# A loop of 13 turns over 56 edge steps on VectorE, or one of 22 turns over 32 steps with 24 steps in line behind it

## The chip, the cores and the metric

The kernel runs on one core of a Trainium2 chip. The metric is the device time of one execution in microseconds (us), lower is better. TensorE is written PE here, as in the profile, VectorE is DVE, ScalarE is ACT, GpSimd is POOL and SyncE is SP.

## The reference

The kernel computes two graph layers with residual normalization over 12500 nodes of 64 features and 400000 edges sorted by target node. Cut to what matters:

```python
def layer0(x, src, dst):                      # mean over in-edges, two small products
    mean = segment_sum(x[src], dst) / maximum(degree, 1)
    return relu(concat([x, mean]) @ W_fc + b_fc) + x @ W_res + b_res

def conv(x, edge_attr, src, dst):             # twice, with a relu between
    msg = x[src] @ Wm + bm + edge_attr @ We + be
    return segment_sum(msg, dst) + x @ Ws + bs

x = layernorm(x + layer0(x, src, dst))
x = layernorm(x + layer1(x, edge_attr, src, dst))   # layer1 = conv, relu, conv
```

Since `edge_attr @ We` is linear, the sum of the edge features over the edges of each node, `segment_sum(edge_attr, dst)`, is needed only once, 400000 rows of 64 floats. That sum is the stage that the change touches.

## The kernel before

The program runs in this order: preparation (the steps and tables are worked out on the chip), round 0 (neighbour sums for layer 0), the **edge sum**, and rounds 1 and 2 (the two convolutions). Each engine has its own instruction stream, written out by hand, with semaphores between them. An engine's sequencer works through the stream, does waits, register sums and branches itself, and hands the tensor operations to the engine.

The edge sum takes the edges in groups of 640 (128 partitions by 5), 625 groups, in 728 steps (`ESTEPS`); a group that reaches over a border of two blocks of 128 nodes takes a step for each block. The 8 buffers of a step's data turn round (`EB = 8`, `h` is the step modulo 8). One step passes through five engines:

- SP (L1540) loads 160 KB of edge features into `feats`.
- POOL (L1291) writes `rel_e`, the target node of each edge less the first node of the block.
- DVE (L921) compares it with a row of lane numbers and so marks, 128 by 640, which edge belongs to which node of the block (`mark_e`).
- ACT (L1416) turns the marks of two steps into floats (`hot_e`).
- PE (L1179) multiplies features by marks into one PSUM bank of 8, five products in a step.
- DVE (L932) adds the bank of the step six before (`LAG = 6`) to the block's sum in `sums_e`.

So DVE does two tensor operations in each step, L921 and L932. The block that L932 adds to is one of 98 and is known only at run time. `load_blocks` (L463 to L471) reads it into the sequencer's registers: one TENSOR_LOAD reads 32 bit words, each with four block numbers. In the stream one `load_blocks` stands ahead of every 16 steps (four words), and where fewer than 16 steps are left of the loop's body, for those alone (8 steps, two words).

The stage's loops on the other engines have 91 turns of 8 steps (PE, ACT, POOL) or 13 turns of 56 (SP, `TURNS = 7`). On DVE the loop (L913) has 13 turns of 56 steps. Behind it DVE adds the last six banks (L938), and PE then folds the sums (L1188). Every engine goes on to round 1 from there.

Of the kernel before, what the change touches and what calls it, by code (L numbers as in the profile page):

```python
# [105 lines left out]
def gnn_program(nc, step_c, first_row, x, src, dst, edge_attr, W_fc, b_fc, W_res, b_res,  # L106
# [26 lines left out]
    EB = 8  # L133
    LAG = 6
    EDGE0 = LAG % 4
    ESTEPS = -(-(GROUPS + BLOCKS - 1) // EB) * EB
    TURNS = 7
    assert ESTEPS % (EB * TURNS) == 0
    ES = -(-(ESTEPS + 1) // P)
    NB = 7  # L140
# [30 lines left out]
    with ctx:  # L171
# [291 lines left out]
        def load_blocks(frm, n):  # L463

            words = steps[0:1, :].bitcast(I32)
            _, packed = nc.values_load_multi_w_load_instructions(  # L466
                words[0:1, bass.ds(frm, n // 4)], engines=(ENG.DVE,), min_val=0,
                max_val=(BLOCKS - 1) * 0x01010101,
                skip_runtime_bounds_check_because="four block numbers, each clamped when the path was made")
            return [nc.s_assert_within(b, 0, BLOCKS - 1, skip_runtime_bounds_check_because="one of the four block numbers")  # L470
                    for v in packed for b in (v & 0x7F, (v >> 8) & 0x7F, (v >> 16) & 0x7F, v >> 24)]  # L471

        def flat(v):
            return v.rearrange("p b d -> p (b d)")
# [3 lines left out]
        def _(dve):  # L478
# [58 lines left out]
            for b in range(-(-CG // CH)):  # L537
                cols = slice(b * CH, min(b * CH + CH, CG))
                n = cols.stop - cols.start
# [90 lines left out]
            for b in range(3):  # L630
                cols = slice(b * GP, min(b * GP + GP, SG))
                n = cols.stop - cols.start
# [66 lines left out]
            for c0, c1, landed in ((0, SG // 2, s_g[0]), (SG // 2, SG, s_last)):  # L699
                dve.wait_ge(landed, 16 * (c1 - c0))  # L700
                n, cols = c1 - c0, slice(c0 * P, c1 * P)
# [25 lines left out]
            for r in range(3):  # L727
# [82 lines left out]
                if r == 0:  # L810
# [5 lines left out]
                    for b0, blocks, wd, deeps, s0 in REG:  # L816
                        upto, pair = steps_upto(wd, deeps)
                        many = at_once(wd)
                        with dve.Fori(0, blocks // 2) as i:
                            for j in range(2):  # L820
# [3 lines left out]
                                for q in range(upto[j][0], upto[j][WPB]):  # L824
                                    n, s = q % RING, bass.ds(i * pair + (q + s0), many)
# [11 lines left out]
                                    if part == 0:  # L837
                                        dve.wait_ge(b_used[j], it + (1 + j))
                                        if b0 < 2 * GI:
                                            bs = load_blocks((it * 2 + j) * (GW // 4), GW)  # L840
# [69 lines left out]

                step(V.memset(ps[:, EB - LAG:EB, 0:P], 0.0), "zeros_e")
                first_block = SETS * GW + GW + EDGE0 - LAG
                with dve.Fori(0, ESTEPS // EB, TURNS) as turn:  # L913
                    for n in range(EB * TURNS):
                        i, h = turn + n // EB, n % EB
                        if n % (2 * EB) == 0:
                            bs = load_blocks(turn * (EB // 4) + (first_block + n) // 4, min(2 * EB, EB * TURNS - n))
                        if h % 2 == 0:
                            dve.wait_ge(e_hot[h // 2], i + 1)
                        dve.wait_ge(e_rel[h], i + 1)  # L920
                        marks = V.tensor_tensor(mark_e[:, h, :, :].rearrange("p j (c u) -> p j c u", u=2),  # L921
                                                lane16[:, 0:P].rearrange("p (c u) -> p c u", u=2).unsqueeze(1)
                                                .to_broadcast([P, EG, P // 2, 2]),
                                                rel_e[:, h, :, :].unsqueeze(2).to_broadcast([P, EG, P // 2, 2]),
                                                ALU.is_equal)
                        if h % 2:
                            marks.then_inc(e_mark[h // 2], 1)
                        b = (h - LAG) % EB
                        dve.wait_ge(e_mm[b], i + (2 if h >= LAG else 1))
                        dve.wait_ge(e_add, i * EB + (h + EB))  # L930
                        to = flat(sums_e[:, bass.ds(bs[n % (2 * EB)], 1), :])
                        V.tensor_tensor(to, to, ps[:, b, 0:P], ALU.add).then_inc(e_add, 1)  # L932
                last = load_blocks((SETS * GW + ESTEPS + GW + EDGE0 - LAG) // 4, EB)
                for k in range(LAG):
                    dve.wait_ge(e_mm[EB - LAG + k], ESTEPS // EB + 1)
# [652 lines left out]
```

## Time and profile before

| | |
|---|---|
| median of 3 runs | 3590.3 us (3588.47 to 3590.58) |
| span of the profiled execution | 3585.2 us, from its first instruction to its last |
| busy in the span | PE 88%, DVE 65%, POOL 56%, ACT 45% |
| edge sum, first mark of DVE to its last | 1536.6 to 2020.2 us |
| TensorE's granted clock in the edge sum | 0.99 of full speed (2.4 GHz) |

The span leaves out what lies ahead of the first instruction and behind the last, so a run's time is some us longer than a span: the median is 5.1 us above this one. In the rows, `DVEq` is the sequencer of DVE: register sums (ALU_OP, FUSED_REGOPS), loads into registers (TENSOR_LOAD) and branches; while it does them no new tensor operation is handed to the engine. "issue" is time in which an engine waited for nothing that the profile shows. A name such as `union` is the memory in which several tiles lie in turn (`mark_e`, `hot_e` and `feats` in this stage); `abuf` holds `sums_e`.

### The profile page before, as it was taken

What the parts mean: (1) busy time and instruction counts of PE and PEld (TensorE: products, weight loads), DVE (VectorE), ACT (ScalarE), POOL (GpSimd) and SP (SyncE); (2) the same over time, 40 slices, a digit from 0 to 9 for tenths busy, and PEclk for the clock granted to TensorE, in tenths of its full rate; (3) what the DMA queues carried; (4) which work ended last, traced back from release to release, by engine and by line L of the source; (5) the groups of instructions that cost most, each with busy time, mean ns of one, the idle gap of its engine ahead of it and who ended that gap; (6) DMA issues with size and microseconds to landing.
All of it is one profiled execution on the core that took longest, in us unless ns stands there. A gap on an engine that the chain in (4) does not pass through costs nothing.

```text
span 3585.2 us, 114923 instructions
## 1 busy us (share of the span) xinstructions
PE 3167.6 (88%) x39408; PEld 2958.1 (83%) x39408; DVE 2339.3 (65%) x5369; ACT 1613.7 (45%) x2096; POOL 2021.8 (56%) x2292
## 2 busy tenths in 40 slices
PE   0239999999999999889999889999999889999995
PEld 0127988888888888778888879999999889999995
DVE  8779998888888888779999682333333423333335
ACT  0123677878999999788988650000000400000000
POOL 6761234445666666534444256666666666666664
PEclk9869999999999999999999979999999999999998
DMA  3521455556666666668888429999999599999996
GB/s 92 134 18 70 167 194 198 218 213 233 238 240 251 251 238 240 245 207 247 248 246 247 147 93 400 403 402 402 402 402 403 202 354 403 402 402 402 402 402 241
DMA packets 232872, 959.10 MB, mean 268 GB/s; under 512 B 44815, under 2 KB 144285, under 8 KB 173818
## 3 DMA queue, kind: packets, MB, share of 16 engines
q1 hardware_dynamic: 186027, 884.48, 65.0%
q0 software_dynamic: 46784, 73.84, 6.8%
q8 instruction: 33, 0.54, 0.1%
q14 instruction: 28, 0.23, 0.0%
HBM read 694.75 MB, written 263.40 MB: 267 GB/s over the span
## 4 chain that ended last, share of the span: by engine, by line
PE 68%; DVE 11%; issue 8%; POOL 6%; DVEq 3%; ACT 2%; DMA 2%; SPq 0%; ACTq 0%; POOLq 0%
PE ps L1109 48%; PE ps L1132 10%; DVE union L805 5%; PE ps L1179 4%; PE ps L1101 3%; POOL abuf L1213 3%; DVE union L921 2%; ACT union L1416 1%; DVE abuf L932 1%; POOL union L1213 1%; PE ps L1069 1%; DVEq L466 1%; DVEq L932 1%; PE ps L1188 1%; POOL abuf L1255 0%
## 5 line engine op out<-in xcount | busy, mean ns | idle before, releaser
L1271 POOL DMA_INDIRECT msg<-y_tab,idx x1368 | 1531.1, 1119 | 1041.9 <-ACT idx L1377 652.0
L1109 PE MATMUL ps<-union,abuf 128*128 128x192 bf16 x14896 | 1265.3, 247 | 13.9 <-DVEq L782 10.2
L1109 PEld LDWEIGHTS ps<-union,abuf 128*128 128x128 f16 x14896 | 1226.7, 98 | 21.2 <-issue 10.6
L1398 ACT ACTIVATE abuf<-ps 128x784 f16<-128x784 f32 x1216 | 1000.7, 823 | 239.9 <-PE ps L1132 212.3
L805 DVE TENSOR_TENSOR union<-lane,union 128x1568 f16<-128x1568 f16 (+3 forms) x1440 | 949.5, 710 | 31.0 <-PE ps L1132 27.1
L1109 PE MATMUL ps<-early,abuf 128*128 128x195 bf16 x7546 | 853.4, 249 | 0.0
L1109 PEld LDWEIGHTS ps<-early,abuf 128*128 128x128 f16 x7546 | 677.1, 99 | 100.9
L1132 PE MATMUL ps<-union 128*128 128x392 f16 (+2 forms) x4288 | 689.5, 288 | 52.4 <-DVE union L805 47.1
L1377 ACT ACTIVATE idx<-src_g 128x6 int32 (+1 forms) x228 | 46.4, 205 | 1280.2 <-PE ps L1101 1277.9
L1179 PE MATMUL ps<-union 128*64 128x128 f32 x7280 | 444.4, 278 | 48.2 <-ACT union L1416 48.1
L1179 PEld LDWEIGHTS ps<-union 128*64 128x64 f32 x7280 | 394.1, 137 | 98.4 <-DVE abuf L932 79.2
L1416 ACT ACTIVATE union<-union 128x1280 f32<-128x1280 f16 x364 | 432.9, 1259 | 55.9 <-DVE union L921 53.9
L797 DVE TENSOR_TENSOR acc<-acc,ps 128x64 f32 (+1 forms) x918 | 203.7, 222 | 364.2 <-DVE acc L797 211.2
L1132 PEld LDWEIGHTS ps<-union 128*128 128x128 f16 x4288 | 362.9, 108 | 92.3 <-issue 48.3
L921 DVE TENSOR_TENSOR union<-lane,rel_e 128x640 f16<-128x640 f16 x728 | 352.5, 484 | 41.7 <-issue 40.3
L1291 POOL TENSOR_TENSOR rel_e<-early,base_e 128x10 f16 x728 | 208.4, 305 | 287.5 <-DVE union L921 271.1
L880 DVE TENSOR_REDUCE part_d<-ps 128x64 f32<-128x192 f32 x152 | 54.4, 358 | 459.2 <-PE ps L1109 459.2
L786 DVE TENSOR_TENSOR hot_g<-code_g,lane 128x768 f16<-128x768 f16 x228 | 218.0, 956 | 70.2 <-DVE acc L797 69.2
L932 DVE TENSOR_TENSOR abuf<-abuf,ps 128x128 f32 x728 | 203.5, 280 | 1.8 <-PE ps L1179 1.1
L1101 PE MATMUL ps<-msg,hot_g 128*128 128x64 bf16 (+1 forms) x4104 | 167.2, 194 | 5.5 <-DMA msg<-y_tab,idx 5.5
L1101 PEld LDWEIGHTS ps<-msg,hot_g 128*128 128x128 f16 x4104 | 157.0, 98 | 6.0 <-DMA msg<-y_tab,idx 6.0
L854 DVE TENSOR_TENSOR acc<-acc,ps 128x65 f32 x456 | 99.5, 218 | 56.8 <-DVE acc L854 37.9
(229 smaller groups left out, 1241.4 us busy)
## 6 DMA issues: line engine op xcount, KB each, us to landing
abuf<-a_dram SPq DMA_DIRECT2D x304, 1568.0 KB
a_dram<-abuf SPq DMA_DIRECT2D x76, 3136.0 KB
union<-in_edge_attr_dram SPq DMA_DIRECT2D x728, 160.0 KB, 2.9
msg<-y_tab,idx POOLq DMA_INDIRECT x1368
y_tab<-union SPq DMA_DIRECT2D x28, 336.0 KB, 2.2
abuf<-in_x_dram SPq DMA_DIRECT2D x28, 224.0 KB, 3.4
y_tab<-early SPq DMA_DIRECT2D x7, 682.5 KB, 5.5
out_dram<-union SPq DMA_DIRECT2D x2, 800.0 KB, 3.5
```

The costliest lines, as they stand in the source:

```text
L786: V.tensor_tensor(hot_g[:, j * G:(j + 1) * G, :], code_g[:, bass.ds((it * 2 + j) * G, G)].unsqueeze(2).to_broadcast([P, G, P]), lane16[:, ...
L805: return V.tensor_tensor(to.rearrange("p s (c u) -> p s c u", u=2), lanes.unsqueeze(1).to_broadcast([P, n, width // 2, 2]), codes[:, which ...
L921: marks = V.tensor_tensor(mark_e[:, h, :, :].rearrange("p j (c u) -> p j c u", u=2), lane16[:, 0:P].rearrange("p (c u) -> p c u", u=2).uns ...
L932: V.tensor_tensor(to, to, ps[:, b, 0:P], ALU.add).then_inc(e_add, 1)
L1101: last = nc.tensor.matmul(tile_ps(r, j, k), hot_g[:, s, :], msg[:, s, c * width_of[r]:(c + 1) * width_of[r]], start=c == 0, stop=c == 2)
L1109: last = nc.tensor.matmul(ps[:, bank, 0:3 * width_of[r]], abuf[:, buffer, hi * P:(hi + 1) * P], ycols[r][:, hi, :], start=hi == 0, stop=hi ...
L1132: nc.tensor.matmul(ps[:, w % 4, 0:WIN].rearrange("p (h d) -> p h d", d=WD)[:, :, d0:d0 + wd], hot_c[:, n, WIN:WIN + P], hot_c[:, n, 0:HIS ...
L1179: last = nc.tensor.matmul(ps[half:half + D, h, 0:P], feats[:, h, j * D:(j + 1) * D], hot_e[:, h, j, :], start=j < 2, stop=j >= EG - 2)
L1271: pool.indirect_dma_start(msg[:, s, 0:3 * width_of[r]], None, y_tab[r], bass.IndirectOffsetOnAxis(ap=idx[:, s:s + 1], axis=0)).then_inc(ga ...
L1291: nc.gpsimd.tensor_tensor(rel_e[:, h, :, :], flat(dst_e[:, bass.ds(grp[h], 1), :]).unsqueeze(2) .to_broadcast([P, EG, 2]), base_e[:, bass. ...
L1398: A.activation(abuf[:, j, :].rearrange("p (h w d) -> p w h d", w=WPB, d=WD) [:, w:w + 2, :, :], ps[:, w % 4:w % 4 + 2, 0:WIN].rearrange("p ...
L1416: A.activation(hot_e[:, h:h + 2, :, :], mark_e[:, h:h + 2, :, :], ACT.Copy)\
```

## The change

The body of the DVE loop becomes a function of a first turn and a number of turns of 8 steps. The loop now takes 4 such turns (`HELD`), 32 steps, and goes round 22 times; the 24 steps that are left stand behind it in line, with numbers in place of registers where the turn is known. The steps themselves, their order and their semaphores stay as they are, on DVE and elsewhere; SP keeps its body of 56 steps.

```diff
     TURNS = 7
+    HELD = 4
...
-                with dve.Fori(0, ESTEPS // EB, TURNS) as turn:
-                    for n in range(EB * TURNS):
+                def edge_steps(turn, turns):
+                    for n in range(EB * turns):
                         i, h = turn + n // EB, n % EB
                         if n % (2 * EB) == 0:
-                            bs = load_blocks(turn * (EB // 4) + (first_block + n) // 4, min(2 * EB, EB * TURNS - n))
+                            bs = load_blocks(turn * (EB // 4) + (first_block + n) // 4, min(2 * EB, EB * turns - n))
...
+                whole = ESTEPS // EB // HELD * HELD
+                with dve.Fori(0, whole, HELD) as turn:
+                    edge_steps(turn, HELD)
+                edge_steps(whole, ESTEPS // EB - whole)
                 last = load_blocks((SETS * GW + ESTEPS + GW + EDGE0 - LAG) // 4, EB)
```

Two places of the DVE stream show it. The first is the foot of the loop. Before, the last step of the body (the mark L921, the sum L932) is followed by the loop's branch (L913) and then by what stands behind the loop, the load and the first of the six closing sums (L938):

```order
L921 TENSOR_TENSOR union<-lane16,rel_e 128x640 [waits e_rel7]
L930 REGISTER_ALU [waits e_mm1]
L932 ISA [waits e_add]
L932 TENSOR_TENSOR abuf<-abuf,ps 128x128
L913 REGISTER_ALU
L913 COMPARE_AND_BRANCH
L466 TENSOR_LOAD steps
L938 REGISTER_ALU [waits e_add,e_mm2]
L938 ISA
L938 TENSOR_TENSOR abuf<-abuf,ps 128x128
```

Now the same foot (lines are one higher, the loop is L936) is followed by the first of the steps in line, which has its load, its mark (L922) and its sum (L933):

```order
L922 TENSOR_TENSOR union<-lane16,rel_e 128x640 [waits e_rel7]
L931 REGISTER_ALU [waits e_mm1]
L933 ISA [waits e_add]
L933 TENSOR_TENSOR abuf<-abuf,ps 128x128
L936 REGISTER_ALU
L936 COMPARE_AND_BRANCH
L467 TENSOR_LOAD steps
L922 TENSOR_TENSOR union<-lane16,rel_e 128x640 [waits e_rel0,e_hot0]
L933 REGISTER_ALU [waits e_add,e_mm2]
L933 ISA
L933 TENSOR_TENSOR abuf<-abuf,ps 128x128
```

In DVE's listing the loop has 312 rows from its head to its branch before and 179 now, and the steps in line are 104 rows; the branch is met 13 times before and 22 times now. The second place is a load inside the body, on DVE, at step 48 of the 56 before; it reads two words for the last 8 steps, with a register sum for its address (L466 ISA) ahead of it:

```order
L932 TENSOR_TENSOR abuf<-abuf,ps 128x128
L466 ISA
L466 TENSOR_LOAD steps
L921 TENSOR_TENSOR union<-lane16,rel_e 128x640 [waits e_rel0,e_hot0]
L930 ISA [waits e_mm2]
```

In the new body the load stands at step 16 and reads four words, as the one at the head does:

```order
L933 TENSOR_TENSOR abuf<-abuf,ps 128x128
L467 ISA
L467 TENSOR_LOAD steps
L922 TENSOR_TENSOR union<-lane16,rel_e 128x640 [waits e_rel0,e_hot0]
L931 ISA [waits e_mm2]
```

So each turn has two loads of four words in place of three of four and one of two; a load of two words is left only once, ahead of the last 8 steps in line.

## Rows read from the trace of the kernel before

**Rows 1.** The page: the chain of work that ended last, by engine.

```profile
PE 68%; DVE 11%; issue 8%; POOL 6%; DVEq 3%; ACT 2%; DMA 2%; SPq 0%; ACTq 0%; POOLq 0%
```

**Rows 2.** Busy time by stretch, edge sum: length, engines, granted clock, DMA share, GB/s.

```profile
1536.00:2021.00 485.00, 441.88 (x7240) 391.97 (x7240) 442.16 (x1456) 431.94 (x364) 208.44 (x728) 0.99 0.81 246
```

**Rows 3.** Groups, 1612 to 2020 us: count, busy us, mean ns, idle before, releaser.

```profile
L1179 PE MATMUL ps<-union 128*64 128x128 f32 x6154 | 374.0, 277 | 34.4 <-ACT union L1416 34.4
L1416 ACT ACTIVATE union<-union 128x1280 f32<-128x1280 f16 x309 | 367.2, 1259 | 42.7 <-DVE union L921 41.0
...
L921 DVE TENSOR_TENSOR union<-lane,rel_e 128x640 f16<-128x640 f16 x616 | 298.2, 484 | 35.0 <-issue 35.0
...
L932 DVE TENSOR_TENSOR abuf<-abuf,ps 128x128 f32 x616 | 172.2, 279 | 0.0
```

**Rows 4.** Who waited for whom, 1612 to 2020 us: total us, times, longest.

```profile
DVE union L921 <- issue: 35.0, 44, 1.3
```

**Rows 5.** DVE in order of time, one turn: start, us, operation, idle before it.

```profile
1613.52 0.49 DVE L921 TENSOR_TENSOR union<-lane,rel_e 128x640 f16<-128x640 f16 x1 [1.25 <-issue]
...
1633.02 0.48 DVE L921 TENSOR_TENSOR union<-lane,rel_e 128x640 f16<-128x640 f16 x1
...
1634.49 0.49 DVE L921 TENSOR_TENSOR union<-lane,rel_e 128x640 f16<-128x640 f16 x1 [0.79 <-issue]
...
1643.51 0.48 DVE L921 TENSOR_TENSOR union<-lane,rel_e 128x640 f16<-128x640 f16 x1
...
1644.53 0.49 DVE L921 TENSOR_TENSOR union<-lane,rel_e 128x640 f16<-128x640 f16 x1 [0.34 <-issue]
...
1648.14 0.48 DVE L921 TENSOR_TENSOR union<-lane,rel_e 128x640 f16<-128x640 f16 x1
...
1648.74 0.48 DVE L921 TENSOR_TENSOR union<-lane,rel_e 128x640 f16<-128x640 f16 x1
...
1650.67 0.49 DVE L921 TENSOR_TENSOR union<-lane,rel_e 128x640 f16<-128x640 f16 x1 [1.24 <-issue]
```

**Rows 6.** DVE's register loads, 1612 to 2020 us: ns min/median/max, first and last.

```profile
L466 DVEq TENSOR_LOAD <-steps x44: 520/965/985, 1612.4 to 2015.3; - x44
```

**Rows 7.** The chain at one turn of the edge loop: start us, us, what.

```profile
1649.11 0.06 DVEq L913
1649.17 0.26 DVE abuf L932
1649.42 0.06 DVEq L913
1649.48 0.04 issue
1649.52 0.96 DVEq L466
1650.48 0.04 issue
1650.52 0.04 DVEq L919
```

**Rows 8.** The chain at one turn of a round 0 loop of DVE (L819).

```profile
608.00 0.06 DVEq L819
608.05 0.23 issue
```

**Rows 9.** Instruction transfers in the first two turns, 1536 to 1610 us: packets, MB, share.

```profile
q14 instruction: 3, 0.02, 0.1%
```

**Rows 10.** All DMA queues with packets, 1610 to 2020 us.

```profile
q1 hardware_dynamic: 89067, 101.38, 81.3%
```

**Rows 11.** DVE in order of time, in the first turn.

```profile
1562.97 0.29 DVE L932 TENSOR_TENSOR abuf<-abuf,ps 128x128 f32 x1 [0.18 <-issue]
```

**Rows 12.** The chain in the closing sums behind the loop.

```profile
2022.48 0.43 issue
```

**Rows 13.** PE in order of time, inside a turn.

```profile
1647.20 4.90 PE L1179 MATMUL ps<-union 128*64 128x128 f32 x80 [0.33 <-ACT union L1416]
```

**Rows 14.** PE in order of time, behind the stage.

```profile
2025.28 22.10 PE L1188 MATMUL ps<-twofold,abuf 128*128 128x64 f32 x196 [1.73 <-DVE abuf L938]
```

## Prediction

> **What bounds the kernel now.** I read the chain of work that ended last, then the stage that the change touches, since shares over the whole span say little about one stage. Over the span the chain is PE's for 68% and DVE's for 11%, and DVE's sequencer and "issue" hold 3% and 8% of it [rows 1]. In the edge sum all is dense at once: of 485 us PE is busy 442, DVE 442, ACT 432 and the DMA engines 81%, at a granted clock of 0.99 [rows 2]. Which of them sets the pace is read from what each waits for in the steady part, 1612 to 2020 us. PE's matmuls were idle 34.4 us, ended by ACT; ACT 42.7 us, of which DVE's marks ended 41.0; DVE's marks 35.0 us, all of them "issue", and DVE's sums not at all [rows 3]. So the chain of causes ends at DVE, and DVE waits for no other engine. It waits for its own sequencer, 44 times in 11 turns of the loop, which is four times a turn [rows 4].
>
> The timeline shows where these are [rows 5]. A plain step takes 0.60 us from one mark to the next (1648.14 to 1648.74). Four of the 56 steps of a turn take longer. Inside the body, a step ahead of which `load_blocks` reads four words takes 1634.49 - 1633.02 = 1.47 us, 0.87 more; the one with two words takes 1644.53 - 1643.51 = 1.02 us, 0.42 more; and the step over the loop's edge, which has the branch and a load of four words, takes 1650.67 - 1648.74 = 1.93 us, 1.33 more. A turn is then 56 x 0.60 + 1.33 + 2 x 0.87 + 0.42 = 37.1 us, and the trace has 1650.67 - 1613.52 = 37.15 us. Nothing is left over that the loads and the edge don't explain.
>
> PE could go faster, but not by much: where it runs without a gap, 80 of its instructions (8 steps, ten each) take 4.90 us, 0.61 us a step [rows 13]. DVE's mean with its stalls is 37.15 / 56 = 0.66. A DVE stall of this size is therefore paid by the stage, and a DVE without any would at best meet PE at 0.61.
>
> **The change part by part.** *The loads.* They hold DVE's sequencer 965 ns each in the median, 520 ns for the short ones [rows 6], and no mark can be handed out meanwhile. Before, 13 turns have three loads of four words and one of two: 39 long, 13 short. Now 22 turns have two long ones each, 44, and the steps in line one long and one short: 45 long, 1 short. That is 6 x 0.87 = 5.2 us more and 12 x 0.42 = 5.0 us less, so +0.2 us. Four words cost twice what two cost, and the number of words is the same, 182.
>
> *The loop's edges.* An edge costs what its step has over one with a long load: 1.93 - 1.47 = 0.46 us [rows 5]. The chain shows what it is made of: the branch ends at 1649.17, the next instruction of the sequencer begins at 1649.42 (the chain names the sum that DVE still does meanwhile), the load only at 1649.52, and behind the load comes one more register instruction at 1650.52 [rows 7]. The last branch of a loop goes on to the code behind it and is there before and now, so the count goes from 12 taken branches to 21: 9 x 0.46 = +4.1 us. What the body's length does to the price of an edge is not shown by this loop. The nearest row is a loop of round 0 on DVE, of 153 rows or more: there the sequencer goes on 0.23 us behind the branch [rows 8], as here (0.25). So I take the same 0.46 for the new body of 179 rows. Lower bound: the 0.23 us behind the branch vanish, which leaves 0.23 an edge, 21 x 0.23 - 12 x 0.46 = -0.7 us. Upper bound: each turn also crosses into code that isn't there yet, below.
>
> *Instruction transfers.* This is where a shorter body could matter. In the first two turns three packets come on the instruction queue of 8 KB packets [rows 9], and in the eleven turns from 1610 to 2020 us none: the queue of edge features is the only one with packets [rows 10]. The body of 312 rows is thus held already, and there is no fetch to save. The Trainium skill (Runtime: NRT & Kernel Launch, Instruction fetch mechanics) has it that an engine other than PE holds two blocks of 256 instructions, and that a taken branch to a target outside them waits for a fetch. By that rule a body over 256 could pay at each edge and one of 179 not; the rows speak against it here, since such a fetch would be a packet.
>
> Where code is first entered there is a small pause: 0.18 us idle in the first turn [rows 11], 0.43 us behind the loop [rows 12]; that these are waits for code is my reading, no row names their cause. The code of the stage has 312 rows before and 179 + 104 now, so no more of these are due: 0, at most two of 0.43 where the borders fall badly, +0.9 us.
>
> *The steps in line.* 24 steps keep their two tensor operations, which take 0.60 us a step whatever the sequencer does beside them. Register sums ahead of waits go, but these lie under the operations: nothing. If that cover were gone it would be a saving. Ahead of the two loads the sum for the address (0.06 us) goes: -0.1 us.
>
> *Who is behind DVE.* The marks come later at each added edge, then ACT's floats, then PE's products, which keep 0.05 us a step to spare (0.66 less 0.61). Nothing queues across the end of the stage: PE's fold (L1188) had waited 1.73 us for DVE's last sum [rows 14], and round 1 follows from it. What DVE loses reaches the end in full. SP, POOL, ACT and PE keep their streams; DMA has 19% to spare.
>
> **Sum.** +0.2 + 4.1 - 0.1 = +4.2 us. The profiled execution has a span of 3585.2 us, so 3589.4 us now. The median of the runs lies 5.1 us above that span, for what is ahead of the first instruction and behind the last, and I leave that as it is: 3594.5 us, 0.12% over before. Differences under 0.2% (7.2 us) can hardly be told from no change by a measurement of this kernel.
>
> **The rivals.** *The jump gets cheaper.* A shorter body might leave no pause behind the branch: the lower bound above, with the loads and addresses -0.6 us, 3589.7 us. For it: the pause is the largest part of an edge. Against: DVE's shorter loop has the same pause [rows 8].
>
> *The edge holds a fetch wait now.* Then the rule above would gain: the edge would fall by a pause of 0.43 [rows 12] to 0.03 us, 21 x 0.03 - 12 x 0.46 = -4.9, with the rest -4.8 us, 3585.5 us. Against: no instruction packet in eleven turns [rows 10]. Even without any price at all the edges could give only 12 x 0.46 = 5.5 us back, so this change has hardly a way to be faster by 0.2%.
>
> *A fetch at each turn.* This is the other side, slower by over 0.2%. The place is the foot of the new loop, with the steps in line right behind it: running towards the branch, the sequencer may call for the code behind it and lose the code at the head. The price would be a pause of 0.43 us at each of 21 edges, 21 x (0.46 + 0.43) - 12 x 0.46 = 13.2 us, 3603.5 us. It decides from an edge of (7.2 + 5.5) / 21 = 0.60 us on. For it: such pauses exist [rows 11, 12], and where the borders between blocks of code lie in the new stream isn't known. Against: the longer body shows none in steady state, and it has code behind it too.
>
> *Hidden.* PE sets the pace and takes up the nine edges: 3590.3 us. For it: PE and DVE are both busy for 442 us. Against: DVE's sums never waited for PE in 616 steps [rows 3].
>
> **How the numbers follow.** The forecast has 0.76, the cheaper jump 0.09, the gain by a fetch 0.03, a fetch at each turn 0.08, hidden edges 0.04. The range goes from the cheaper jump, 3589.5, over the forecast with both pauses of 0.9 us and a scatter of 1 to 2 us as the runs before have it, to an edge of 0.65 us, 3598.5 us; it leaves out the fetch at each turn, the gain by a fetch and some 0.07 of the forecast's own scatter. Within 0.2% are most of the forecast (0.69), the cheap jump, the hidden edges and most of the gain: 0.84. Slower by more: the fetch at each turn and 0.06 of the forecast, 0.14. Faster by more: 0.02.
>
> **What would show it.** In the trace of the changed kernel the step over the edge takes 1.93 us as before and comes 21 times, 19.2 + 1.33 + 0.87 = 21.4 us apart; loads take 965 ns; plain steps 0.60 us; the edge sum from first to last mark is 487.7 in place of 483.6 us. Wrong would be: an edge far from 1.93 us, instruction packets that come with each turn, DVE's sums waiting for PE, a pause over 1 us where the steps in line begin, or other stages that change their length by more than a microsecond or two.

## The result, and the profile after

| | before | after |
|---|---|---|
| median | 3589.5 us (3584.9 to 3608.6, 14 runs) | 3612.2 us (3608.4 to 3615.9, 14 runs) |
| ratio | | 1.0056 (95%: 1.0045 to 1.0068) |
| span of the profiled execution | 3585.2 us | 3613.0 us |

The changed kernel is slower: by 0.56% by the ratio, and by 22.7 us or 0.63% by the medians (the three long runs of before, below, pull the ratio down). Predicted was +4.2 us. In three of its 14 runs the kernel before took 3606 to 3609 us, and in the other eleven 3585 to 3592; this gap of some 17 us turns out to be the matter itself.

The loop does what was predicted. The timeline of DVE's marks (start, us, what; idle before in brackets) has, over two edges of the loop and over the place where the loop ends:

```profile
1775.03 0.48 DVE L922 TENSOR_TENSOR union<-lane,rel_e 128x640 f16<-128x640 f16 x1
1776.97 0.49 DVE L922 TENSOR_TENSOR union<-lane,rel_e 128x640 f16<-128x640 f16 x1 [1.25 <-issue]
...
1798.39 0.49 DVE L922 TENSOR_TENSOR union<-lane,rel_e 128x640 f16<-128x640 f16 x1 [1.26 <-issue]
...
2012.24 0.49 DVE L922 TENSOR_TENSOR union<-lane,rel_e 128x640 f16<-128x640 f16 x1 [0.87 <-issue]
2012.85 0.48 DVE L922 TENSOR_TENSOR union<-lane,rel_e 128x640 f16<-128x640 f16 x1
2013.50 0.49 DVE L922 TENSOR_TENSOR union<-lane,rel_e 128x640 f16<-128x640 f16 x1
2014.15 0.49 DVE L922 TENSOR_TENSOR union<-lane,rel_e 128x640 f16<-128x640 f16 x1
2014.75 0.49 DVE L922 TENSOR_TENSOR union<-lane,rel_e 128x640 f16<-128x640 f16 x1
...
2015.69 0.48 DVE L922 TENSOR_TENSOR union<-lane,rel_e 128x640 f16<-128x640 f16 x1
...
2022.00 0.49 DVE L922 TENSOR_TENSOR union<-lane,rel_e 128x640 f16<-128x640 f16 x1
...
2023.01 0.49 DVE L922 TENSOR_TENSOR union<-lane,rel_e 128x640 f16<-128x640 f16 x1 [0.33 <-issue]
...
2027.42 0.48 DVE L922 TENSOR_TENSOR union<-lane,rel_e 128x640 f16<-128x640 f16 x1
```

An edge takes 1776.97 - 1775.03 = 1.94 us, as [rows 5] had 1.93, and the next is 1798.39 - 1776.97 = 21.42 us later. In the steps in line some pitches are 0.60 us (2014.15 to 2014.75) and others 0.65 (2012.85 to 2013.50, 2013.50 to 2014.15). That was not expected. The 23 pitches from 2012.24 to 2027.42 take 15.18 us. At 0.60 us a step, with the one load among them (two words, 0.42 us [rows 5], ahead of 2023.01; the load of four words lies ahead of 2012.24), they would take 14.22; 0.96 us are over. Twelve pitches of 0.65 us are 0.6 of it. The other 0.34 is a single pitch of 0.94 us, 2014.75 to 2015.69, in which the sequencer, in the chain of waits, stands still between two register sums:

```profile
2014.98 0.40 issue
```

It waits there for nothing that the profile shows. This is the kind of small pause that the prediction reads as code entered for the first time.

From 1600 to 2010 us, the waits of DVE, its loads (min/median/max ns) and the DMA queues (packets, MB, share) read as [rows 4, 6 and 10] do:

```profile
DVE union L922 <- issue: 38.9, 38, 1.3
```

```profile
L467 DVEq TENSOR_LOAD <-steps x38: 959/966/980, 1604.4 to 2000.6; - x38
```

```profile
q1 hardware_dynamic: 88184, 100.38, 81.9%
```

Two loads a turn in 19 turns, of four words each; no queue of instructions has a packet, so no fetch comes with a turn; and DVE waits for nothing but its own sequencer.

The time is lost behind the edge sum. The timeline of PE at the end of that stage and the start of round 1 (last products, fold, first products of round 1):

```profile
2025.68 5.08 PE L1185 MATMUL ps<-union 128*64 128x128 f32 x80 [0.30 <-DVE abuf L933]
...
2032.38 39.76 PE L1194 MATMUL ps<-twofold,abuf 128*128 128x64 f32 x196 [1.61 <-DVE abuf L944]
2076.26 6.31 PE L1075 MATMUL ps<-w_in,abuf 65*128 65x128 f32 x28 [4.12 <-DMA abuf<-in_x_dram]
```

The fold, the same 196 products, takes 39.76 us where [rows 14] have 22.10. It waited no longer for DVE than before (1.61 us against 1.73), and its products follow one another without a gap. What differs is the clock. The busy time of the engines in stretches around the fold (length; busy us of PE, of its weight loads, of DVE, ACT and POOL; granted clock; DMA share; GB/s):

```profile
2027.00:2032.40 5.40, 3.79 (x61) 3.19 (x61) 2.88 (x11) 2.18 (x2) 0.00 (x0) 1.00 0.11 39
2032.40:2035.00 2.60, 2.60 (x23) 2.60 (x24) 0.98 (x2) 0.59 (x1) 0.00 (x0) 0.99 0.00 0
2035.00:2045.00 10.00, 10.00 (x49) 10.00 (x49) 0.00 (x0) 1.80 (x4) 0.00 (x0) 0.50 0.01 2
2045.00:2072.20 27.20, 27.14 (x128) 26.95 (x127) 0.00 (x0) 4.80 (x9) 0.00 (x0) 0.50 0.00 0
```

and in the profiled execution of the kernel before, the same columns, over the fold and from just behind it:

```profile
2025.30:2036.00 10.70, 10.70 (x96) 10.70 (x97) 0.97 (x2) 2.98 (x5) 0.00 (x0) 1.00 0.01 2
2036.00:2047.40 11.40, 11.38 (x102) 11.24 (x101) 0.00 (x0) 4.01 (x7) 0.00 (x0) 1.00 0.00 0
2049.50:2100.00 50.50, 45.77 (x196) 42.78 (x196) 40.54 (x69) 7.50 (x13) 15.74 (x17) 0.50 0.22 63
```

Before, TensorE kept 2.4 GHz through the whole fold and fell to 1.2 GHz only in the pause behind it. Now it falls at 2035.0 us, 2.6 us into the fold, behind a pause of 1.61 us, and the rest of the fold runs at 1.2 GHz.

The two profiled spans differ by 27.8 us, in order of the program: the edge sum starts 1.95 us later (1538.59 against 1536.64; the stages ahead of it are not touched); from its first mark to its last 488.83 against 483.56 us, +5.27; from the last mark to the fold 4.95 against 5.09, -0.14; the fold 39.76 against 22.10, +17.66; all that follows +3.0. The edge sum and the fold are together 22.9 us, as the medians have it (22.7). The 1.95 us ahead and the 3.0 us behind lie within the scatter of single executions: with the same code ahead of it the edge sum starts at 1537.2 us in the trace of e4 below and at 1539.2 in that of e13, and behind the fold e13, the changed kernel once more, took 1536.4 us, where it is 1540.9 here and 1537.9 in the kernel before.

### The profile page after: what moved, and what is told of

It is laid out like the page before. It is cut to its first block, busy times and chain, and to the rows that moved or that the text cites. A ratio compares the mean times of both kernels' runs of the same rounds, so it can differ in the third digit from the quotient of the medians.

```text
span 3613.0 us, 114933 instructions
## 1 busy us (share of the span) xinstructions
PE 3186.5 (88%) x39408; PEld 2977.2 (82%) x39408; DVE 2340.0 (65%) x5369; ACT 1615.5 (45%) x2096; POOL 2033.3 (56%) x2292
## 4 chain that ended last, share of the span: by engine, by line
PE 68%; DVE 11%; issue 7%; POOL 6%; DVEq 3%; DMA 2%; ACT 2%; SPq 0%; ACTq 0%; POOLq 0%
PE ps L1115 47%; PE ps L1138 10%; DVE union L806 5%; PE ps L1185 5%; PE ps L1107 3%; POOL abuf L1219 3%; DVE union L922 2%; ACT union L1422 2%; DVE abuf L933 1%; POOL union L1219 1%; PE ps L1194 1%; DVEq L467 1%; PE ps L1075 1%; DVEq L933 1%; DMA abuf<-in_x_dram 1%
## 5 line engine op out<-in xcount | busy, mean ns | idle before, releaser
L922 DVE TENSOR_TENSOR union<-lane,rel_e 128x640 f16<-128x640 f16 x728 | 354.0, 486 | 46.5 <-issue 45.1
L933 DVE TENSOR_TENSOR abuf<-abuf,ps 128x128 f32 x728 | 204.9, 282 | 2.2 <-PE ps L1185 1.6
```

## The experiments

When I say below that the fold fell, I mean that it ran at half clock. Every profiled execution shows directly whether it did. The other runs fall for most kernels into two clusters of time some 17 us apart, and the mean granted clock on record for each run sorts them in the same way: 0.959 to 0.963 where the fold fell, 0.965 or more where it didn't. (e3 and e10, whose clock falls in the edge sum too, go by time and trace alone, and so do the first 14 runs of the kernel before, for which no clock is on record.) The runs of an experiment were taken together with runs of the kernel before on one chip; I call this a group. Ratios and counts are compared within a group, since the share in which the kernel before falls moved from group to group: 3 of 14 beside the changed kernel, 6 of 28 (e1 to e4), 8 of 30 (e5 to e8), 4 of 17 (e9, e10), 17 of 23 (e11, e12) and 3 of 22 (e13 to e15). The chip alone doesn't explain it: 8 of 30 and 17 of 23 were on the same chip.

Three theories were to be told apart. **A**: the end of the edge sum decides, that is how PE is fed in the last steps and how long it idles just ahead of the fold; in its narrowest form (A1) the pace of 0.65 us in the steps in line does it. **B**: the 21 edges spread over the stage do it. **C**: the moment at which the stage ends does it.

### 1. e1_lead_in: the 24 steps in line ahead of the loop

```diff
+                lead = ESTEPS // EB - whole
+                edge_steps(0, lead)
+                with dve.Fori(lead, ESTEPS // EB, HELD) as turn:
+                    edge_steps(turn, HELD)
```

> The changed kernel with the 24 steps in line ahead of the loop in place of behind it; the 22 turns and their edges stay. Theory A (the steps in line, being the last before the fold, are what costs TensorE its clock): the edge sum stays about 5 us longer than in the kernel before, the fold (L1188 there) runs at full clock, 22 us, and the time is +5 us or +0.15%. Theory B (more edges make TensorE less busy over the whole stage and so cost it the clock): the fold takes 40 us, +23 us. Theory C (any shift of the stage's end by a few us does it): +23 us as well.

Measured: 3598.9 us against 3590.2, ratio 1.0019 (1.0003 to 1.0035); the fold fell in 1 run of 12. PE's fold in its trace:

```profile
2035.16 22.10 PE L1195 MATMUL ps<-twofold,abuf 128*128 128x64 f32 x196 [1.73 <-DVE abuf L945]
```

The edge sum took 490.2 us, and a turn 21.52: its edge is 1.96 us and one more of its steps takes 0.68. So the edges cost what they should, +6.6 us for the stage with the steps in line at its head, and the fold stays whole. (The time is 8.6 us over by the medians; the 2 us beyond the stage were not followed up.) As many edges in the loop, another order: B in its plain form, any edges anywhere in the stage, falls.

### 2. e2_last56: twelve turns of 56 steps and the last 56 in line

```diff
+                whole = (ESTEPS // EB // HELD - 1) * HELD
+                with dve.Fori(0, whole, HELD) as turn:
+                    edge_steps(turn, HELD)
+                edge_steps(whole, ESTEPS // EB - whole)
```

with `HELD = 7`.

> The loop of before with its body of 56 steps, 12 turns, and the last 56 steps in line behind it: one taken edge less than before, no added load. In line a step took about 0.64 us in the changed kernel, so 56 of them cost some +2 us. Theory A: the fold falls to half clock, 40 us, and the time is +19 to +20 us. Theory B (edges): fold 22 us, +1 to +2 us. Theory C (shift): +2 us is a smaller shift than in the changed kernel, so rather +2 us.

Measured: 3610.9 us, 1.0050 (1.0036 to 1.0064); the fold fell in 11 of 11. No edge is added here (the edge sum took 486.1 us, +2.6 for the steps in line alone), and yet:

```profile
2029.91 40.82 PE L1194 MATMUL ps<-twofold,abuf 128*128 128x64 f32 x196 [1.25 <-DVE abuf L944]
```

Steps in line at the end are enough, with one edge less than before. The pause ahead of the fold is shorter here (1.25 us) than in the trace of before (1.73): its length alone does not tell which fold falls.

### 3. e3_body104: seven turns of 104 steps, none in line

```diff
+    HELD = 13
-        steps = sb("steps", [1, GW + STEPS + 4], U8)
+        steps = sb("steps", [1, GW + STEPS + 128], U8)
```

> A body of 104 steps with 7 turns and nothing in line: 6 taken edges in place of 12, loads 42 long and 7 short. If the price of an edge is 0.46 us and the code is held, the edge sum is 2.7 us shorter and the time -3 us with the fold at full clock (all theories). If 524 rows are more than DVE holds, instruction packets come in each turn; with a pause of 0.4 us for each of some four packets a turn it is +8 us or more.

Measured: 3625.1 us, 1.0084 (1.0061 to 1.0107). Not fewer edges made it slow but what each cost. A mark behind an edge, and the queue of 8 KB packets between 1700 and 1950 us:

```profile
1763.18 0.49 DVE L922 TENSOR_TENSOR union<-lane,rel_e 128x640 f16<-128x640 f16 x1 [4.78 <-issue]
```

```profile
q14 instruction: 22, 0.18, 0.3%
```

Six edges of 5.5 to 6.3 us, with packets in each turn: the edge sum is 36.9 us longer, 23 us of it in these edges (over 1.93 us each), the rest mainly in smaller pauses inside the turns. This is the fetch at each turn that the prediction had as a rival, at eight to ten times its price, for a body too long to be held. The Trainium skill (Runtime: NRT & Kernel Launch, Instruction fetch mechanics) says that a taken branch to a target outside the two blocks at hand waits for a fetch; the trace agrees here, and an edge costs 3.5 to 4.4 us more than a held one. The fold fell in none of 6 runs. TensorE's clock had been down in this stage by then, for 6.8 us behind five of its six edges, as here:

```profile
1763.00:1770.00 7.00, 4.16 (x40) 4.17 (x42) 5.63 (x18) 4.86 (x4) 2.49 (x8) 0.52 0.24 76
```

### 4. e4_after_fill: the changed kernel, and 14 products on PE ahead of the fold

```diff
+                    for _ in range(14):
+                        nc.tensor.matmul(ps[:, 0, 256:256 + P], ident[:, :], ident[:, :], start=True, stop=True)
                     pe.wait_ge(e_add, ESTEPS + LAG + EB)
```

Nothing reads their output; they only keep PE at work where it would wait for DVE's closing sums. (The trace shows each of them as two records.)

> The changed kernel with 14 products of the unit matrix with itself on TensorE between its last edge step and the fold, into a part of a PSUM bank that nobody reads: TensorE has work in the 1.6 us in which it waits for DVE's closing sums. If the pause in front of the fold is part of what costs the clock, the fold runs at full clock, 22 us, and the time is +5 us over before, -18 us against the changed kernel. If the clock falls for what came earlier, in the steps themselves, the fold stays at 40 us and the time at +23 us.

Measured: 3592.3 us, 0.9993 (0.9978 to 1.0009); the fold fell in 0 of 12.

```profile
2028.59 3.39 PE L1190 MATMUL ps<-ident 128*128 128x128 f32 x28
2031.82 22.00 PE L1196 MATMUL ps<-twofold,abuf 128*128 128x64 f32 x196
```

The edge sum is as in the changed kernel (488.2 us), and the 14 products outlast the wait, so that the fold starts 6.50 us behind the last mark in place of 4.95. It takes 22.00 us all the same. With PE at work in the pause the fold doesn't fall: the loss beyond the edge sum needs PE's idle time at this seam. (The time is 2.1 us over before by the medians, less than the longer stage and the later fold would make it; that rest wasn't followed up.)

### 5. e5_tail_loop and e14_tail_loop_again: the last 24 steps as a loop of one turn

```diff
-                edge_steps(whole, ESTEPS // EB - whole)
+                with dve.Fori(whole, ESTEPS // EB, ESTEPS // EB - whole) as turn:
+                    edge_steps(turn, ESTEPS // EB - whole)
```

The steps stay where they are, with registers in place of constants.

> The changed kernel with its last 24 steps as a loop of a single turn in place of code in line, so that they use registers as the other turns do; edges and order stay as in the changed kernel. Theory A1 (the steps in line are slower, 0.65 us where the loop has 0.60, and this pace just ahead of the fold costs the clock): the steps go back to 0.60 us, the edge sum is about 4.5 us longer than before and the fold takes 22 us: +4 to +5 us over before. Rival A2 (any 24 steps behind 22 turns, by the moment at which the stage ends): the fold stays at 40 us, +22 us.

Measured: 3608.0 us (3594.4 to 3613.3), 1.0029 (1.0009 to 1.0049); the fold fell in 7 of 12, where that of the kernel before beside it fell in 8 of 30. Its 23 pitches are back at 14.41 us, 0.60 a step, and the profiled run fell:

```profile
2031.03 39.67 PE L1195 MATMUL ps<-twofold,abuf 128*128 128x64 f32 x196 [1.72 <-DVE abuf L945]
```

Pause and pace are here those of the kernel before, and the fold fell nevertheless. The same kernel was run again in the last group:

> As e5: the last 24 steps as a loop of one turn with registers, at 0.60 us a step. Theory A1: the share of before, well under that of e13. Rival D: no difference between e13, e14 and before.

Measured: 3611.7 us, 1.0044 (1.0029 to 1.0059); 10 of 11 fell, of before 3 of 22. With the pace at 0.60 us most folds still fall: A1 is not the only cause.

### 6. e6_pause: the kernel before, with a longer pause

```diff
+                for _ in range(3):
+                    step(V.memset(rdeg[:, :], 1.0))
                 last = load_blocks((SETS * GW + ESTEPS + GW + EDGE0 - LAG) // 4, EB)
```

Three small operations of DVE, each waited for, stand between the loop and the closing sums.

> The kernel before, with three small memsets on VectorE between the loop and the closing sums, each waited for: TensorE's pause in front of the fold grows from 1.7 to about 2.7 us and nothing else changes. If the pause is part of what costs the clock, the fold falls to half clock in most runs and the time is +1 us from the pause and +18 us from the fold, +19 us. If only the pace of the steps ahead counts, +1 us.

Measured: 3610.1 us, 1.0038 (1.0019 to 1.0058); the fold fell in 11 of 12 (before: 8 of 30).

```profile
2028.58 39.82 PE L1190 MATMUL ps<-twofold,abuf 128*128 128x64 f32 x196 [2.56 <-DVE abuf L940]
```

Loop and steps are those of the kernel before, the edge sum takes 483.8 us, and 0.83 us more of waiting make the fold fall nearly always. So the seam decides without any change of the loop.

### 7. e7_fills: the kernel before, with products ahead of and behind the fold

```diff
+                    for _ in range(6):
+                        nc.tensor.matmul(ps[:, 0, 256:256 + P], ident[:, :], ident[:, :], start=True, stop=True)
                     pe.wait_ge(e_add, ESTEPS + LAG + EB)
...
                         last.then_inc(e_fold, 1)
+                    for _ in range(15):
+                        nc.tensor.matmul(ps[:, 7, 256:256 + P], ident[:, :], ident[:, :], start=True, stop=True)
```

> The kernel before, with products of the unit matrix on TensorE in its two pauses: 6 ahead of the fold (about 1.4 us) and 15 behind it (about 3.6 us of the 4 us in which it waits for features of round 1). If pauses cost the clock, none of the runs has the 17 us more that 6 of 28 runs of before show, and the clock stays up behind the fold for at least some products of round 1, which take 6.3 us for 28 at half clock: -5 to -18 us. If they don't, no change.

Measured: 3584.4 us, 0.9975 (0.9958 to 0.9991); 0 of 12 fell. This one beats both kernels. About half of the gain over before is that no fold falls: against those 22 runs of before whose fold was whole (median 3588.8 us) it is 4.4 us, or 0.12%.

```profile
2024.02 1.60 PE L1184 MATMUL ps<-ident 128*128 128x128 f32 x12
2025.83 22.10 PE L1190 MATMUL ps<-twofold,abuf 128*128 128x64 f32 x196 [0.20 <-DVE abuf L938]
...
2051.99 3.36 PE L1069 MATMUL ps<-w_in,abuf 65*128 65x128 f32 x28 [0.66 <-DMA abuf<-in_x_dram]
2057.21 6.34 PE L1069 MATMUL ps<-w_in,abuf 65*128 65x128 f32 x28 [1.85 <-DMA abuf<-in_x_dram]
```

Six products leave 0.20 us of the pause and don't delay the fold. The 15 behind it carry the clock into round 1: 28 products take 3.36 us at first, and 6.34 from 2057.2 on, where PE has again waited for a load.

### 8. e8_body8: 91 turns of 8 steps

`HELD = 1`, nothing in line.

> A body of 8 steps, 91 turns, nothing in line: 90 taken edges in place of 12, all loads short. With 0.46 us an edge it is 78 x 0.46 - 1.1 = +34.8 us in the edge sum. Theory A: the steps ahead of the fold run at 0.60 us up to it and the fold keeps 22 us: +35 us in all. Theory B (edges make TensorE less busy and cost the clock): the fold takes 40 us, +53 us.

Measured: 3632.6 us, 1.0099 (1.0068 to 1.0131); 4 of 5 fell. The edge sum is 509.8 us, 26.2 more, not the 34.8 expected: a turn is 5.60 us and its edge, with a load of two words, 1.39 us, 0.37 over the step with such a load inside a body [rows 5]. The price of an edge in a short body is a little smaller (0.37 in place of 0.46) but doesn't go away. The folds came out as B forecast for this run and not as A did: steps at 0.60 us up to the end, nothing in line, and yet most fell (before, beside them: 8 of 30), in the trace behind a pause of 1.35 us. Since the 21 edges of e1 did not do this, what is left of B is an edge near the end: the last one stands 8 steps ahead of it here, 32 in e1.

### 9. e9_fills_r1: as e7_fills, and products behind each of the 14 groups of round 1's start

```diff
                         last.then_inc(a_prod, 1)
+                        for _ in range(6):
+                            nc.tensor.matmul(ps[:, 0, 0:P], ident[:, :], ident[:, :], start=True, stop=True)
```

> The kernel before with the products of e7 in TensorE's two pauses and six more behind each of the 14 groups of products at the start of round 1, where e7 still has pauses of 0.2 to 1.9 us and runs at half clock from its second group on. If pauses cost the clock, these groups take 3.4 us each in place of 6.3 and the chain there waits for the features' transfers of 3.2 us instead: -5 us from e7's two pauses and up to -10 us more. If the fall in e7 came from something else, about -5 us as in e7.

Measured: 3583.4 us, 0.9973 (0.9957 to 0.9990); 0 of 12 fell.

```profile
2052.77 1.80 PE L1069 MATMUL ps<-w_in,abuf 65*128 65x128 f32 x14 [0.69 <-DMA abuf<-in_x_dram]
2055.75 1.73 PE L1069 MATMUL ps<-w_in,abuf 65*128 65x128 f32 x14
```

The products of round 1's start run at full clock now (1.73 us for 14, where e7 took 6.34 for 28 later on), but the ratio is that of e7: that PE runs faster there gains nothing.

### 10. e10_shift and e11_after_shift: more code ahead of the edge sum

Into the kernel before (e10) and the changed one (e11), ahead of DVE's loop:

```diff
+                for _ in range(14):
+                    step(V.memset(rdeg[:, :], 1.0))
```

> The kernel before with 14 small memsets on VectorE ahead of the edge loop, each waited for, which shifts the stage by some 5 us and leaves its steps, its end and the pause as they are. Theory A (the pace of the last steps and the pause in front of the fold): +5 us, and the fold falls in about a quarter of the runs, as in before (8 of 30). Theory C (the moment at which the stage ends): the share changes clearly, to none or to most of the runs, which are then 17 us longer.

Measured: 3692.5 us, 1.0277 (1.0246 to 1.0307). The run tells nothing of what it was for, the moment (C), since the loop itself changed. A mark ahead of an edge, the one behind it, and the 8 KB queue from 1700 to 1950 us:

```profile
1711.20 0.48 DVE L923 TENSOR_TENSOR union<-lane,rel_e 128x640 f16<-128x640 f16 x1
1717.47 0.49 DVE L923 TENSOR_TENSOR union<-lane,rel_e 128x640 f16<-128x640 f16 x1 [5.36 <-issue]
```

```profile
q14 instruction: 28, 0.23, 0.3%
```

The body of 56 steps, held in every other trace, now brings packets in each turn, an edge takes 6.0 to 6.6 us, a turn 44.1 us in place of 37.15, and the edge sum 567.3 us, +83.7. Of this the twelve edges hold some 52 us, and pauses inside the turns most of the rest. Fourteen operations ahead of it in the stream, with the body itself as it was, have done this; that they moved it across the borders of what is held is my reading, no row shows these borders.

> The changed kernel with the same 14 small memsets ahead of its loop that e10 puts ahead of the loop of before. In e10 they moved the code of the loop, and its body of 56 steps was no longer held: five instruction packets and 6 to 6.6 us an edge in each turn. If a body of 32 steps is held wherever it lies, no packets come in its turns, an edge stays at 1.94 us, and the time is that of the changed kernel and the memsets, +27 to +30 us over before (3617 to 3621) with the fold at half clock. If a body of 32 steps can fall out as well, 21 edges cost 4.5 us more each: +120 us.

Measured: 3612.4 us, 1.0021 (1.0000 to 1.0042); the fold fell in 9 of 12, of before in 17 of 23 beside it.

```profile
1714.86 0.49 DVE L924 TENSOR_TENSOR union<-lane,rel_e 128x640 f16<-128x640 f16 x1 [1.25 <-issue]
1736.28 0.49 DVE L924 TENSOR_TENSOR union<-lane,rel_e 128x640 f16<-128x640 f16 x1 [1.25 <-issue]
```

Here the body of 32 steps stays held: turns of 21.42 us, no instruction packets. With the same code ahead, the program with the changed loop is 80 us faster than that with the loop of 56 (3612.4 against 3692.5, in two groups). The shorter body buys nothing where the kernel stands, and a good deal where its place in the stream falls badly.

### 11. e12_pool_shift: a later edge sum, with DVE's code where it was

```diff
+                    for n, end in enumerate((HIS, HIS, HIS, HALF + HALF // 2)):
+                        pool.memset(sums_e[:, HALF:end, :], 0.0).then_inc(e_late, 1)
+                        pool.wait_ge(e_late, n + 1)
                     pool.memset(sums_e[:, HALF:HIS, :], 0.0).then_inc(e_zero, 1)
```

POOL clears its part of the sums some more times ahead of the stage, which DVE waits for.

> The kernel before with four more memsets on GpSimd ahead of the edge sum, each waited for, so that VectorE's loop starts some 4 us later with VectorE's code where it was: what e10 was to test. Theory A (pace and pause): the time of before plus 4 us, with the fold falling in about a quarter of the runs (12 of 47 so far in the runs of before beside these experiments). Theory C (the moment at which the stage ends): the share changes clearly, to none or to most.

Measured: 3614.3 us (3596.2 to 3617.1), 1.0026 (1.0003 to 1.0048); 9 of 12 fell, and of before, in the same group, 17 of 23. The stage starts at 1544.4 us in place of 1536.6 and is otherwise the same (483.5 us). The shares are alike. In e1 the fold starts 9.9 us later than in the kernel before (2035.16 against 2025.28), and it fell in 1 run of 12. So a later end does not by itself raise the share, as C would have it; these are two shifts, others were not run.

### 12. e13_after_again and e15_after_swap: the changed kernel again, and with two waits swapped

In the steps in line DVE waits ahead of L933 for the products and for its own last sum. In the kernel e15 these two waits change places there:

```diff
+                        waits = [(e_mm[b], i + (2 if h >= LAG else 1)), (e_add, i * EB + (h + EB))]
+                        for s, v in waits[::-1] if turns < HELD else waits:
+                            dve.wait_ge(s, v)
```

> The changed kernel once more, beside the two below and before on the same chip, for the share of runs in which the fold falls to half clock. Theory A1 (the pace of the steps in line): most or all runs, above the share of before. Rival D (the share moves from chip to chip and from time to time and the steps in line add nothing): the share of before.

Measured: 3611.1 us, 1.0051 (1.0032 to 1.0069); 6 of 6 fell (before: 3 of 22), the edge sum 488.7 us. Rival D, by which the change adds nothing to the share, is not borne out here.

> The changed kernel with the two waits ahead of each sum changed in their order in the steps in line alone (first for DVE's own last sum, then for the bank), so that another of them stands in an instruction by itself. If that instruction is what holds the steps in line at 0.65 us, it may go back to 0.60 us; the edge sum is then 0.8 us shorter. Theory A1: where the pace is 0.60, the share of falls is that of before and e14; where it stays 0.65, that of e13.

Measured: 3603.7 us (3595.9 to 3614.9), 1.0030 (1.0014 to 1.0047); 6 of 12 fell. The profiled fold is whole:

```profile
2031.34 22.10 PE L1195 MATMUL ps<-twofold,abuf 128*128 128x64 f32 x196 [1.53 <-DVE abuf L945]
```

The pitches in line are 0.60 us now. What the swap acts on is seen by a line's instructions on DVE's sequencer (min/median/max ns, first and last start) in the changed kernel. In a turn of the loop, 1775 to 1796 us, the line of the wait for the last sum has the register sums that work out the value to wait for (in the listing of the change these carry the waits):

```profile
L931 DVEq ALU_OP  x28: 40/45/45, 1775.0 to 1795.9; - x28
L931 DVEq FUSED_REGOPS  x4: 53/53/53, 1777.0 to 1792.3; - x4
```

In the 24 steps in line, 2012 to 2028 us, there is nothing to work out, and each step has an instruction there that only waits:

```profile
L931 DVEq EVENT_SEMAPHORE  x24: 21/21/21, 2012.3 to 2027.5; - x24
```

It holds the wait for DVE's last sum, which is the later of the two, and the sums that find the block come behind it. The chain of waits of the changed kernel has them in one of its steps of 0.65 us, behind a sum of DVE that ends at 2023.70:

```profile
2023.42 0.28 DVE abuf L933
...
2023.81 0.04 DVEq L933
...
2023.89 0.04 DVEq L933
...
2023.96 0.06 DVEq L933
```

In a step that needs one register sum less it fits into 0.60. In the kernel e15 the waiting instruction is for the products, it is done while DVE's last sum still runs, and the wait for that sum is carried by the first register sum. The edge sum is hardly shorter (488.4 us), but the fold falls less often than in the changed kernel beside it (6 of 12 against 6 of 6).

## Why the prediction was wrong

- **What bounds the stage**: right. DVE's sequencer sets the pace of the edge sum, and each DVE stall reaches its end: +5.27 us from the first mark to the last.
- **The loads**: right. Two of 966 ns a turn.
- **The loop's edges**: right. 1.94 us each, 21.42 us apart, +4.1 us for nine more; the shorter body didn't make the jump cheaper. Even in the body of 8 steps (e8) 0.37 of the 0.46 us are left.
- **Instruction transfers**: right for this program: no packet comes with a turn before or after. But "the body of 312 rows is thus held already" holds for this place in the stream alone: the same body moved (e10) costs 4.1 to 4.7 us more at each jump, and one of 104 steps (e3) 3.5 to 4.4. The rule that was weighed there, and set aside on the rows, fits these two: both bring packets in each turn.
- **The steps in line**: wrong in size, by 1.0 us. The sum took 24 steps at 0.60 us, with their register work hidden. 23 pitches took 15.18 us where 14.22 were due. Of the difference 0.34 us is the one pause in a pitch of 0.94 us; the sum had such pauses at 0 and its upper bound at two of 0.43. The other 0.6 us are the register sums' doing. The register sums that go had each carried a wait; with constants one of the two waits has an instruction to itself, and where this is the wait for DVE's last sum it stands in the open ahead of the sums for the block: with the waits swapped (e15) or with registers (e5) the pitch is 0.60 again. With both in the sum the stage would have come out at +5.2.
- **Who is behind DVE**: this step failed. "What DVE loses reaches the end in full" is true of the edge sum, but the fold and what follows were put down as unchanged, from one profiled execution in which the fold took 22.10 us. That length is one of two. The fold ran at 1.2 GHz in every run of the changed kernel (14 of 14, 6 of 6) and in 3 of 14 of the kernel before, and this is 17.7 of the 22.7 us. The wait of 1.73 us was read [rows 14] as a sign that nothing queues across the seam; it was in truth a pause of TensorE behind which its clock may fall. The prediction named "other stages that change their length by more than a microsecond or two" as what would make it wrong, and gave that no chance.
- **The rivals**: none came true. The cheaper jump, the gain by a fetch and the hidden edges are excluded by the edge of 1.94 us; a fetch at each turn by the empty queue. The 0.14 for slower by more than 0.2% stood for that fetch and for scatter; the time did come out there, but by neither.
- **From the span to the time of a run**: misread, without harm to the forecast. In all runs with both on record the time is 1.7 to 1.9 us above the span. So of the 5.1 us between the median and the profiled span some 3 were scatter among runs, and not time ahead of the first instruction and behind the last.

What the runs show of the cause: PE's idle time at the seam is needed for the fall. With fills ahead of the fold 0 of 36 runs fell (e4, e7, e9), where 18 of 75 runs of before beside them did; with a pause of 2.56 us 11 of 12 did. Neither edges spread over the stage (e1: 1 of 12) nor a later end (e1, e12) raised the share. How DVE's work ends does: with the loop's exit 24 steps ahead of the end and the steps in line behind it, the fold of the changed kernel fell in 20 of 20, where 6 of 36 runs of before beside it did. In the traces of fallen folds the clock goes down 0.5 to 2.7 us into the fold, while PE works without a gap; so what makes it fall is to be looked for ahead of that.

What stays open: which part of that end does it. The pace of 0.65 us is not needed (e14: 10 of 11; e8: 4 of 5), but with the 24 steps kept at the end and without that pace a smaller share fell in two of three experiments (e5: 7 of 12, e15: 6 of 12). The pause's length alone doesn't sort the kernels, since 1.25 us fell in 11 of 11 (e2), 1.36 in 0 of 6 (e3), and 1.73 in 1 of 12 (e1); and the trace of e11 has a whole fold behind 1.62 us. Nor is it known why the kernel before falls in 3 of 22 runs of one group and 17 of 23 of another, in which the changed kernel with its added operations (e11) fell no more often. A count of falls thus depends on the group, and the median of before (3589.5) is the time of its likelier case and not of a steady one.

## What to carry to other kernels

Where a change moves the end of one stage by little, look at the next stage's clock: a stretch that TensorE runs alone cost 1.8 times as much here when its clock fell at the seam, and some products that nobody needs, put where TensorE waits, kept it up (e4 lies 2.1 us over the kernel before, where the changed kernel lay 22.7 us over it; e7 beats the kernel before by 0.25%). Look at all runs of the kernel before, not at their median alone: two clusters mean that one of its stages has two lengths, and a change may settle which. And a loop's body that is held in one program may not be held in the next, so look at the instruction queue before a long body is lengthened or anything is put ahead of it.

## What the runs showed of the hardware

- The same 196 products took 22.0 to 22.1 or 39.7 to 41.7 us, by whether TensorE's granted clock fell from 1.00 to 0.50 within 2.7 us of the first of them, behind a pause of 1.25 to 2.6 us; products with no gap between them didn't bring it up again before the fold's end.
- A loop body of 56 steps (312 rows of the listing) was held, with no packet in eleven turns, or brought packets in each turn, by nothing but 14 waited-for operations ahead of it. An edge was then 6.0 to 6.6 us in place of 1.93, and the program 103 us longer by the medians (3692.5 against 3589.0), 84 us of it in the edge sum and most of the rest in a fold that fell.
- After all but one of such edges TensorE's granted clock was at half for 6.8 us (e3: five of six; e10: eleven of twelve), so that a jump that isn't held costs PE beyond the jump.
- Two waits on constants cost more than two on registers in twelve of 23 steps, 0.65 us in place of 0.60, and not with the two waits in the other order (e15): by which of the two has an instruction to itself.
